# GpSimd masks the fourth pair and makes the first low matrices of group 1; ScalarE and VectorE make group 2's first half of columns early

## The reference

```python
# x (32, 256, 256), cond (32, 8), weight (8, 256, 256), mask (256, 256), bias (256,)
masked_w = weight * mask[None, :, :]
w_bot = jnp.einsum('bg,got->bot', cond, masked_w)
out = x + jnp.einsum('bnt,bot->bno', x, w_bot) + bias
```

## Time and profile before

| what | us |
|---|---|
| median of 3 runs | 66.35 |
| lowest and highest run | 66.0, 66.44 |
| span of the profiled execution, first to last instruction | 65.5 |
| TensorE busy | 58.8 (90%) |
| VectorE busy | 48.1 (73%) |
| ScalarE busy | 47.9 (73%) |
| GpSimd busy | 7.0 (11%) |

### The profile page before, as it was taken

How to read it: one execution, slowest core, us unless ns; L and a number is a source line. 1 busy time by engine, 2 the same in 40 slices (tenths; PEclk the granted TensorE clock), 3 DMA queues, 4 the chain that set the end, 5 groups by cost and what they waited for, 6 DMA issues and landing times.

```text
span 65.5 us, 1501 instructions
## 1 busy us (share of the span) xinstructions
PE 58.8 (90%) x645; PEld 54.3 (83%) x645; DVE 48.1 (73%) x36; ACT 47.9 (73%) x40; POOL 7.0 (11%) x17
## 2 busy tenths in 40 slices
PE   2997188999999999999999999999999999999910
PEld 1266087977888899999999999999999999999900
DVE  2109809999957989999999999989999992250200
ACT  2506609799889999999999799999869986005520
POOL 5500299900000000000000000000000000000000
PEclk9999999999999999999999999999999999999999
DMA  0999999999998157954999999999999229918393
GB/s 0 260 373 306 352 412 422 407 434 428 420 410 340 60 85 255 408 215 198 245 285 225 400 451 420 403 441 423 398 413 425 93 100 408 398 63 325 158 372 116
DMA packets 5334, 20.21 MB, mean 309 GB/s; under 512 B 592, under 2 KB 1104, under 8 KB 4432
## 3 DMA queue, kind: packets, MB, share of 16 engines
q1 hardware_dynamic: 5040, 19.89, 79.6%
q10 hardware_dynamic: 288, 0.23, 1.1%
HBM read 11.73 MB, written 8.39 MB: 307 GB/s over the span
## 4 chain that ended last, share of the span: by engine, by line
PE 79%; DMA 9%; ACT 4%; SPq 2%; issue 1%
PE slots L433 20%; PE slots L431 20%; PE slots L432 20%; PE slots L451 11%; DMA weights<-in_first 9%; PE slots L332 6%; ACT w_raw L534 3%; PE slots L326 2%; ACT weights L563 1%; SPq L230 1%; SPq L222 1%; SPq L229 1%
## 5 line engine op out<-in xcount | busy, mean ns | idle before, releaser
L431 PE MATMUL slots<-x_hi,w_hi 128*128 128x256 f32 x112 | 31.4, 280 | 0.0
L432 PE MATMUL slots<-x_lo,w_hi 128*128 128x256 f32 x112 | 31.2, 279 | 0.0
L433 PE MATMUL slots<-x_hi,w_lo 128*128 128x256 f32 x112 | 31.2, 279 | 0.0
L431 PEld LDWEIGHTS slots<-x_hi,w_hi 128*128 128x128 f32 x112 | 21.1, 188 | 0.0
L432 PEld LDWEIGHTS slots<-x_lo,w_hi 128*128 128x128 f32 x112 | 21.1, 188 | 0.0
L433 PEld LDWEIGHTS slots<-x_hi,w_lo 128*128 128x128 f32 x112 | 21.1, 188 | 0.0
L589 DVE TENSOR_TENSOR x_lo<-x_ring,x_hi 128x2048 fp32r<-128x2048 f32 (+1 forms) x8 | 16.1, 2022 | 0.5 <-ACT x_hi L491 0.5
L491 ACT CAST x_hi<-x_ring 128x2048 fp32r<-128x2048 f32 (+1 forms) x8 | 13.5, 1694 | 1.3 <-DMA x_ring<-in_x 1.3
L511 ACT ACTIVATE weights<-slots,smalls 128x1024 f32<-128x1024 f32 x10 | 10.8, 1112 | 4.7 <-PE slots L433 4.7
L598 DVE TENSOR_TENSOR w_lo<-w_raw,w_hi 128x2048 fp32r<-128x2048 f32 x6 | 13.7, 2288 | 0.2 <-ACT w_hi L499 0.2
L499 ACT CAST w_hi<-w_raw 128x2048 fp32r<-128x2048 f32 x6 | 11.5, 1909 | 0.0
(11 more groups left out here) (25 smaller groups left out, 19.3 us busy)
## 6 DMA issues: line engine op xcount, KB each, us to landing
out<-weights SPq DMA_DIRECT2D x15, 512.0 KB, 4.7
x_ring<-in_x SPq DMA_DIRECT2D x7, 1024.0 KB, 9.6
x_ring<-in_first SPq DMA_DIRECT2D x6, 512.0 KB, 7.2
weights<-in_first SPq DMA_DIRECT2D x4, 256.0 KB, 6.6
out<-weights SPq DMA_DIRECT2D x1, 256.0 KB, 2.4
out<-weights SPq DMA_DIRECT2D x1, 128.0 KB, 2.3
out<-weights ACTq DMA_DIRECT2D x1, 128.0 KB, 2.1
smalls<-in_small ACTq DMA_DIRECT2D x1, 97.0 KB, 3.1
```

The source lines that it names most:

```text
L431: nc.tensor.matmul(dst, wh, xh, start=(k == 0), stop=False)
L432: nc.tensor.matmul(dst, wh, xl, start=False, stop=False)
L433: last = nc.tensor.matmul(dst, wl, xh, start=False, stop=(k == KC - 1))
```

## The change

GpSimd masks pair 3 as well, after its last slice of unit 1. It then makes the low parts of the first two pieces of group 1 (into `w_lo`, counted by a new semaphore `w_lo_by_pool`). VectorE loses these four instructions. In their place, before unit 6, ScalarE casts the first half of columns of all four batches of group 2 and VectorE takes its difference. ScalarE's two small casts of group 1 move behind the early result's copy, still ahead of unit 6's copy. After unit 7 ScalarE casts x of group 1 before the third piece, and of group 2's weights only the second half is left. SyncE's load of group 3 now waits for GpSimd alone.

```diff
+        def lows_of(g, h):
+            return g + 1 if g > 2 else (None, (None, 2), (1, 3))[g][h]
+        def highs_of(g, h):
+            return g + 3 if g > 2 else (None, (3, 4), (1, 5))[g][h]
...
-            sp.wait_ge(masked_by_pool, 2 * (PAIRS - 2))
-            sp.wait_ge(masked_by_dve, 4)
+            sp.wait_ge(masked_by_pool, 2 * (PAIRS - 1))
             load_group(XS - 1)
...
-            behind_pair = (None, (0,), (1, 2, 3))
-            for j in range(1, PAIRS - 1):
+            behind_pair = (None, (0,), (1, 2, 3), ())
+            for j in range(1, PAIRS):
...
+            for i in range(HO):
+                pool.wait_ge(w_hi_ready, i + 2)
+                nc.gpsimd.tensor_tensor(part(w_lo, 1, *pieces[i]), raw_part(1, *pieces[i]), part(w_hi, 1, *pieces[i]).bitcast(F32),
+                                        ALU.subtract).then_inc(w_lo_by_pool, 1)
...
-                    if u == EARLY and q % 2 == 0:
-                        pe.wait_ge(masked_by_dve, 3 + q // 2)
-                    elif u % 2 == 0 and q % 2 == 0:
+                    if u % 2 == 0 and q % 2 == 0:
                         pe.wait_ge(masked_by_pool, u - 1 + q // 2)
...
-                pe.wait_ge(w_lo_ready, 1 if g == 1 else g + len(pieces) - 1)
+                if g == 1:
+                    pe.wait_ge(w_lo_by_pool, 1)
+                else:
+                    pe.wait_ge(w_lo_ready, lows_of(g, 0))
...
-                            pe.wait_ge(w_lo_ready, 2)
-                        if g == 1 and h == 1 and b == 0:
-                            pe.wait_ge(w_lo_ready, len(pieces))
+                            pe.wait_ge(w_lo_by_pool, 2)
+                        if g <= 2 and h == 1 and b == 0:
+                            pe.wait_ge(w_lo_ready, lows_of(g, 1))
...
                  if u == EARLY:
                     act.wait_ge(raw_masked, 1)
-                    high_piece(0)
-                    high_piece(1)
+                    high_weights(2, 0)
                     act.wait_ge(smalls_loaded, 16)
                     act.wait_ge(early_ready, 1)
                     nc.scalar.activation(result(0, 0)[:, 0:BANK], early, ACT.Identity, bias=bias(0)).then_inc(early_by_act, 1)
+                    high_piece(0)
+                    high_piece(1)
...
-            high_piece(2)
             for lo in (0, NB // 2):
                 high_x(1, lo, lo + NB // 2)
-            high_weights(2)
+            high_piece(2)
             high_x(2)
+            high_weights(2, 1)
...
                  if u == EARLY:
-                    mask_pair(PAIRS - 1)
-                    low_piece(0)
-                    low_piece(1)
+                    low_weights(2, 0)
...
-            low_piece(2)
             for lo in (0, NB // 2):
                 low_x(1, lo, lo + NB // 2)
-            low_weights(2)
+            low_weights(1, 1)
             low_x(2)
+            low_weights(2, 1)
```

More of the change, by code:

```diff
@@ L151, in conditional_residual @@
         w_lo_ready = sem("w_lo_ready")
+        w_lo_by_pool = sem("w_lo_by_pool")
         early_ready = sem("early_ready")
@@ L491, in high_x, with high_weights @@
                 nc.scalar.copy(part_x(x_hi[:, g % RS], lo, hi), part_x(x_ring[:, g % XS], lo, hi)).then_inc(x_hi_ready, 1)
-            def high_weights(g):
+            def high_weights(g, h=None):
                 act.wait_ge(raw_masked, NB * g // MB + 1)
@@ L498, in high_weights @@
                     act.wait_ge(products_ready, HO * (g - RS + 1))
-                nc.scalar.copy(part(w_hi, g), raw_part(g)).then_inc(w_hi_ready, 1)
+                nc.scalar.copy(part(w_hi, g, 0, NB, h), raw_part(g, 0, NB, h)).then_inc(w_hi_ready, 1)
             def high_piece(i):
@@ L524, in _ @@
                     act.wait_ge(raw_by_dve, UNITS // HO)
-                    act.wait_ge(raw_masked, 1)
-                    high_piece(0)
-                    high_piece(1)
+                    high_weights(2, 0)
                     act.wait_ge(smalls_loaded, 16)
@@ L590, in low_x, with low_weights @@
                                         part_x(x_hi[:, g % RS], lo, hi).bitcast(F32), ALU.subtract).then_inc(x_lo_ready, 1)
-            def low_weights(g):
-                dve.wait_ge(w_hi_ready, g + len(pieces) - 1)
+            def low_weights(g, h=None):
+                dve.wait_ge(w_hi_ready, highs_of(g, h))
                 if g > LS:
                     dve.wait_ge(products_ready, HO * (g - LS + 1))
[L598 to L605, removed]
+                nc.vector.tensor_tensor(part(w_lo, g, 0, NB, h), raw_part(g, 0, NB, h), part(w_hi, g, 0, NB, h).bitcast(F32),
                                         ALU.subtract).then_inc(w_lo_ready, 1)
```

## The result

The changed kernel took 66.88 us in the median (11 runs, 66.63 to 69.31), the kernel before 66.38 (11 runs). The ratio is 1.0082, with a 95% interval of 1.0054 to 1.0109: slower by 0.5 us, within the 1% band. 66.8 had been predicted.

What follows compares the result with a forecast made beforehand. TensorE was taken as the bound, its start at 17.75 us held by ScalarE's copy of unit 6. VectorE 0, GpSimd 0, ScalarE's casts 0.47 and later relief 0 gave 66.35 + 0.47 = 66.8 us, range 66.1 to 67.3.

Steps and rivals of the forecast that it cites:

- The bound: TensorE, full from 17.75 us on: whatever moves that start moves the end by as much; later gains elsewhere are worth nothing.
- ScalarE's casts ahead of the copy, 0.47 us: Two small casts delay ScalarE's copy of unit 6 from 16.68 to 17.15, so TensorE starts 0.47 us late.
- the two joints of 0.1: Neighbouring ScalarE rows ahead of unit 6's copy overlap by 0.10 us, twice, giving 17.15 instead of 17.35.
- The median: Whole kernel: median 66.35 + 0.47 = 66.8 us, 0.7% more, within 1% on the slow side.
- VectorE and GpSimd at 0: Their new work around units 6 and 7 and group 1 is ready before TensorE needs it: 0 us each.
- The exclusion of VectorE and GpSimd: VectorE with two SBUF inputs and GpSimd reading SBUF exclude each other; first low piece at 16.75, sum unchanged.
- Rival C: GpSimd is the bound: its group 1 low pieces end too late if over 4.05 us each; chance 0.04.
- The price: GpSimd's low pieces hold TensorE from 4.05 us each; from 1.75 us each they would delay VectorE's low x.
- Rival B: Faster: wider margins remove TensorE's waits at groups 2 and 3; 66.4 to 66.0; chance 0.08 even, 0.04 below 65.7.
- The margins: Slack of VectorE's low parts before TensorE at groups 2 and 3: 0.35 and 0.34 us, growing to about 2.8 and 1.7.

Runs made afterwards that it cites:

- e4: Changed kernel with a third small ScalarE cast, result unused, ahead of unit 6's copy; ratio 1.0126 to the kernel before.
- e2: Changed kernel with the second small cast moved between ScalarE's copies of units 6 and 7; ratio 1.0015 to the kernel before.
- e3: Changed kernel with both small casts moved behind ScalarE's copy of unit 7; ratio 1.0023 to the kernel before.
- e5: Changed kernel with unit 6's copy in two halves, TensorE waiting for the first, casts still ahead; ratio 0.9957 to the kernel before.
- e10: Second run of the changed kernel with unit 6's copy in two halves and casts still ahead; ratio 1.0005 to the kernel before.
- e6: Changed kernel with the masks of pair 3 given back to VectorE; ratio 1.0044 to the kernel before.
- e7: Kernel before with one part of the change alone, GpSimd masking pair 3 instead of VectorE; ratio 1.0025 to the kernel before.
- e8: Changed kernel with both casts behind unit 7's copy, unit 6's copy in halves, pair 3's masks on VectorE; ratio 0.9988 to the kernel before.
- e12: Changed kernel with three repeated 128x512 differences added to GpSimd's low pieces; ratio 1.0157 to the kernel before.
- e11: Second run of the changed kernel with casts behind unit 7's copy, split copy, masks on VectorE; ratio 1.0041 to the kernel before.
- e1: Changed kernel run again with no edit, for a trace beside the others; ratio 1.0072 to the kernel before.

## Why the prediction was right, and where not

- **The bound.** Right. TensorE has no idle row behind the start of the rest of group 0, in before and after, and moving that start by 0.44 and 0.96 us (after, and e4: 3.30 - 2.34) moved the end: the rest stayed at 44.66 or 44.67.
- **ScalarE's casts ahead of the copy, 0.47 us.** Measured 0.44, with the two joints of 0.1 that it took. Taking one cast away (e2), both (e3), adding one (e4) and letting TensorE wait for half of the copy (e5, e10) all moved the start as this step says (in e2 the late mask took 0.29 of it back in the traced execution). This is shown, and it was the whole of the loss that can be resolved.
- **The median.** 0.44 us is 0.66%; measured were 0.82% and 0.72%, with intervals that reach down to 0.54% and 0.38%. Whether 0.1 us more belongs to GpSimd's masks in executions in which pair 3 lands late stays open: e2's trace shows one such case, and the intervals of e6 and e7 are too wide.
- **VectorE and GpSimd at 0.** Right. GpSimd's 128x512 cost 1.28 us, between the bounds of 1.2 and 1.42.
- **The exclusion of VectorE and GpSimd.** The prediction gave it no effect on this change, and in the trace it had none: GpSimd's pieces began as VectorE's low part ended (18.19 against 18.20) and were through before its next (20.70 against 21.62). But it looked only at GpSimd's low pieces. Where pair 3 lands late, GpSimd's masks also run beside VectorE's low weights of group 2, which took 1.71 us in e2 and 1.45 in e4 instead of 1.23; TensorE did not wait for that. VectorE was blocked by GpSimd in e3 (2.17 us instead of 1.2), e7 and e8, GpSimd by VectorE in e12 (2.26 instead of 1.28). The Trainium skill's sentence on two SBUF inputs ("SBUF — State Buffer", Who interferes with whom) is borne out by these rows, in both directions.
- **Rival C's point was wrong.** It asked for over 4.05 us a piece, 8.1 us of GpSimd work. e12 reached TensorE with 6.4. The price had VectorE blocked by GpSimd, and left out that GpSimd is blocked by VectorE in turn, twice for about 0.9 us here. It also looked for trouble only in pieces that last long; in e8 and e11 pieces of 1.28 us that merely come later already hold TensorE, by 0.18 us.
- **Rival B's ground was wrong.** The 0.85 us between median and span were taken for possible waits. Every run since stands some 1.8 us above its span (66.66 and 64.9, 66.64 and 64.8, 67.59 and 65.8). By that, the trace of before, at 65.5, was one of an estimated 67.3 us, later in its loads: the weights that its chain waits for land at 8.29, in e3 at 7.31. The margins did widen as forecast (in e1 the low x of group 2 is ready at 25.09 for a product at 28.02, 2.9 us), and it brought nothing. A wait of the kind that the rival meant is seen once, in e7, and it is 0.07 us.

## What to carry to other kernels

Work that is moved off the busy engines gains only where the bounding engine waits for it; what decides is the queue position of the one instruction it does wait for, so the idle time just ahead of that instruction is a budget, here 0.48 us against 1.13 us of casts put in. Put filler work behind such a copy, or let the waiter wait for the part it needs, and then look at what the filler feeds: in e8 and e11 the casts behind the copies put GpSimd's pieces beside VectorE's low x, and TensorE waited for that. Before giving VectorE's two-input work to GpSimd, lay both engines' two-input stretches beside each other: where they meet, their times add.

## What the runs showed that was not expected

TensorE's products in groups 1 to 7 run at one of two paces at the same granted clock. Windows of TensorE from 24 to 60 us, first e1, then e3 (length, busy with count, clock, DMA):

```profile
24.00:60.00 36.00, 36.00 (x311) 1.00 0.83 320
```

```profile
24.00:60.00 36.00, 36.00 (x308) 1.00 0.83 318
```

One product starts every 0.1167 us in the one and every 0.1178 in the other, which over 336 products is 0.37 us: the whole excess of e3's rest (45.04 - 44.67). e11 changed from the first to the second at 33 us and lost 0.28 us by it; e8 and e7 had the second for some 3 us, worth 0.03. No wait stands in these rows, and DMA moved about the same (320 and 318 GB/s). What sets the pace was not found. It appeared in kernels in which TensorE's start of the rest was not held by ScalarE's lateness, but not in all of them (before, e2, e5 and e10 have the first), so it may be chance. At 0.37 us it is as large as most gains that were sought here.
